# Latent attention on one core: the two score products take three pairs of accumulation banks in turn

## The chip, the cores and the metric

The kernel runs on one core of one Trainium2 chip. The metric is the device time of one execution in microseconds (us). The core has a matmul engine (TensorE, in profiles PE, with its weight loads as PEld), a vector engine (VectorE, DVE), an activation engine (ScalarE, ACT), a general engine (GpSimd, POOL) and a queue for transfers (SyncE, SP).
## The reference, cut to what matters

On a sequence of 2048 tokens by 128 features: half of a six-layer windowed stack, then a latent attention, then the windowed stack again. Only the latent attention is touched.

```python
x = x + 0.5 * _L0_ffn_ref(_layernorm(x), ...)      # six layers, window 32
x = x + _L0_attn_ref(_layernorm(x), ...)           # the latent attention
x = x + 0.5 * _L0_ffn_ref(_layernorm(x), ...)

# _L0_attn_ref, 16 heads; 8 content and 32 rope numbers a head
q = jnp.concatenate([q_content, q_rope], axis=-1)  # 40 numbers a head
k = jnp.concatenate([k_content, k_rope], axis=-1)
scores = jnp.einsum('bhqd,bhkd->bhqk', q, k) * scale
scores = jnp.where(causal[None, None], scores, jnp.float32(-jnp.inf))
attn = jax.nn.softmax(scores, axis=-1)
out = jnp.einsum('bhqk,bhkd->bhqd', attn, v)
return out.transpose(0, 2, 1, 3).reshape(Bx, Tx, N_HEAD * HEAD_DIM) @ W_o
```

## The kernel before

The 16 heads are taken as 8 pairs. The two heads of a pair lie on partitions 0 to 63 and 64 to 127 of `qT` and `kT`: 32 rope rows, one row (32) that holds minus the row maximum in `qT` and one in `kT`, and 8 content rows, so 41 rows in use (`QS = 41`). Rows 41 to 63 were filled once, with 0 in `qT` and with 1 in `kT`, and nothing else writes them. Everything is fp32.

Each pair goes through two score products.

- `scores(pair, y)`, 36 items a pair: queries on the output's partitions, keys along the free axis. VectorE's `maxima` reduces the item to row maxima (line 1455 and neighbours) and signals `s_read`. The maxima of a group of 512 queries are turned into a row by `maxima_turned` and copied to row 32 of `qT`.
- `keyed(pair, t)`, 36 items a pair: the product the other way round, keys on partitions, with minus the maximum already inside. ScalarE's `exps` (line 1374) takes the exponential into `ptl`, four buffers deep, and signals `exped_l`. `outputs` multiplies `ptl` by the values; `summed` normalises a finished group.

An item is one of four kinds: F (a full 128 by 512 block for both heads), D (the diagonal blocks, with the causal mask added by a bf16 matmul first), A and B (the rest of the diagonal group, 384 columns).

Banks before: `keyed` and `exps` use banks 0 to 1 and 2 to 3 in turn (`bank = 2 * (t % 2)`); `scores` and `maxima` have banks 4 and 5 alone, except that the first 18 items of pair 0 (`AHEAD = 18`), before the main loop, go round all three pairs of banks. Bank 6 collects the outputs. Bank 7 is shared by `rope` (line 1170), `maxima_turned` (1211) and `summed` (1280), each of which VectorE must have read before the next may start (`bank_free`).

The order on TensorE is written out by hand. Step t of a pair's 36 issues `keyed(t)`; a rope product for the next pair where t is a multiple of 4 up to 28; `maxima_turned` at t = 5, 19, 22, 29; `summed` at t = 2, 7, 13, 25; `outputs` after t-1 where a unit ends there; and `scores` 18 items ahead. VectorE's order is: rope (three multiplications, lines 1443 and 1446), turned row (1473), normalisation, maxima. ScalarE's is: exps, at t = 1 two long clears of a row (line 1387), copy of a finished group.

The waits of the main loop before: `scores` item n waits until item n-1 is reduced (`s_read`); `keyed` step t waits until exps of step t-2 are done (`exped_l`, which starts at 2); `outputs` at step t waits for the exps of step t-1.

Of the kernel before, what the change touches and what calls it, by code (L numbers as in the profile page):

```python
# [56 lines left out]
QS = QD + 1  # L57
RMS_EPS = 1e-6
PAIRS = HEADS // 2
# [848 lines left out]
def latent_attention(nc, z, i, c, q0, x_res, x_a, x_b, ident, ident_h, causal, mean_w, ones_w, neg_half, zeros):  # L908

    VW = CD + 1  # L910
    with ExitStack() as st:
        def sb(name, shape, dt=F32):
            return st.enter_context(nc.sbuf_tensor(name, shape, dt))
# [28 lines left out]
        ptl = sb("ptl", [P, 4, 2, GT])  # L942
# [29 lines left out]
        NI = 36  # L972
# [3 lines left out]
        AHEAD = 18  # L976
# [32 lines left out]
            return (pair + ahead, y) if pair + ahead < PAIRS else None  # L1009

        def score_bank(pair, y):
            return (4, 0, 2)[y % 3] if pair == 0 and y < AHEAD else 4

        def last_unit(u):
            return u + 1 == len(units) or units[u + 1][0] != units[u][0]
# [90 lines left out]
        def _(pe):  # L1107
# [39 lines left out]
            for n in range(G):  # L1147
# [10 lines left out]
                for m in range(4):  # L1158
                    t = 4 * n + m
# [5 lines left out]
            def rope(pair, j):  # L1165
# [3 lines left out]
                src = qc[:, n * GT:(n + 1) * GT] if w == "q" else x_a[:, 1 + n * GT:1 + (n + 1) * GT]  # L1169
                pe.matmul(ps[:, 7, :], ws[w][:, :], src, start=True, stop=True).then_inc(z["a_ready"], 1)  # L1170

            def heads_rows(h):
                return slice(64 * h, 64 * h + QS)

            def scores(pair, y):
                g, kind = s_items[y][0:2]
                b, bank, early = pair % 2, score_bank(pair, y), pair == 0 and y < AHEAD
                if y == first[g]:
                    pe.wait_ge(z["roped"], pair * 2 * NR + 4 * (g + 1))
                if y == 0:  # L1180
                    pe.wait_ge(z[f"qk_rows_{b}"], 64 * (pair // 2 + 1))
                    if pair >= 1:
                        pe.wait_ge(z["rows_cleared"], 2 * pair)
                if not early:
                    pe.wait_ge(z["s_read"], pair * NI + y)
                elif y >= 3:
                    pe.wait_ge(z["s_read"], y - 2)
                if kind == "D":
                    for h in range(2):
                        pe.matmul(ps[:, bank + h, :], ident_h[:, :], causal[:, :].unsqueeze(1).to_broadcast([P, 4, P]),  # L1190
                                  start=True, stop=False, skip_group_check=True)
                    for t in range(4):
                        for h in range(2):
                            cols = slice((4 * g + t) * P, (4 * g + t + 1) * P)
                            mm = pe.matmul(ps[:, bank + h, t * P:(t + 1) * P], qT[heads_rows(h), b, cols], kT[heads_rows(h), b, cols],
                                           start=False, stop=True, skip_group_check=True)
                else:
                    k0 = s_items[y][3] * GT if kind == "F" else g * GT
                    parts = {"F": lambda: ((s_items[y][2], 0, GT),), "A": lambda: ((4 * g + 1, 0, P), (4 * g + 2, P, 2 * P)),
                             "B": lambda: ((4 * g + 3, 0, 3 * P),)}[kind]()  # L1200
                    for r, lo, w in parts:
                        for h in range(2):
                            mm = pe.matmul(ps[:, bank + h, lo:lo + w], qT[heads_rows(h), b, r * P:(r + 1) * P], kT[heads_rows(h), b, k0:k0 + w],
                                           start=True, stop=True, skip_group_check=True)
                mm.then_inc(z["s_ready_l"], 1)
# [9 lines left out]
            def keyed(pair, t):  # L1215
                b = pair % 2
                g, kind = t_items[t][0:2]
                if t == first[g]:
                    pe.wait_ge(z["m_read"], pair * 2 * G + 2 * (g + 1))
                pe.wait_ge(z["exped_l"], pair * NI + (t + 1))  # L1220
                bank = 2 * (t % 2)
                if kind == "D":
                    for h in range(2):
                        pe.matmul(ps[:, bank + h, :], causal[:, :], ident_h[:, :].unsqueeze(1).to_broadcast([P, 4, P]),
                                  start=True, stop=False, skip_group_check=True)
                    for n in range(4):
                        for h in range(2):
                            cols = slice((4 * g + n) * P, (4 * g + n + 1) * P)
                            mm = pe.matmul(ps[:, bank + h, n * P:(n + 1) * P], kT[heads_rows(h), b, cols], qT[heads_rows(h), b, cols],
                                           start=False, stop=True, skip_group_check=True)  # L1230
                else:
                    parts = {"F": lambda: ((t_items[t][2], 0, 0, GT),), "A": lambda: ((4 * g + 1, 2 * P, 0, 2 * P), (4 * g + 2, 3 * P, 2 * P, P)),
                             "B": lambda: ((4 * g, P, 0, 3 * P),)}[kind]()
                    for kt, q0, lo, w in parts:
                        for h in range(2):
                            mm = pe.matmul(ps[:, bank + h, lo:lo + w], kT[heads_rows(h), b, kt * P:(kt + 1) * P],  # L1236
                                           qT[heads_rows(h), b, g * GT + q0:g * GT + q0 + w], start=True, stop=True, skip_group_check=True)
                mm.then_inc(z["t_ready"], 1)

            def outputs(pair, u):  # L1240
                b = pair % 2
                g, js = units[u]
                pe.wait_ge(z["exped_l"], pair * NI + (js[-1] + 3))
                if u == 0:
                    pe.wait_ge(z["vp_ready"], (pair + 1) * VS)
                if u == 0 or units[u - 1][0] != g:
                    pe.wait_ge(z["osb_ready"], pair * G + (g + 1))

                def add(h, kt, j, src, q0, w, start):
                    strip = 2 * h + kt % 2  # L1250
                    return pe.matmul(ps[32 * strip:32 * strip + 32, 6, q0:q0 + w], vp[:, b, h, kt, :], ptl[:, j % 4, h, src:src + w],
                                     start=start, stop=True, skip_group_check=True)

                for j in js:
                    kind = t_items[j][1]
                    if kind == "F":
                        kt = t_items[j][2]
                        for h in range(2):
                            mm = add(h, kt, j, 0, 0, GT, kt < 2)
                    elif kind == "D":  # L1260
                        if g == 0:
                            for h in range(2):
                                pe.matmul(ps[64 * h + 32:64 * h + 64, 6, 0:P], zeros[:, 0:32], ptl[:, j % 4, h, 0:P],
                                          start=True, stop=True, skip_group_check=True)
                        for n in range(4):
                            for h in range(2):
                                mm = add(h, 4 * g + n, j, n * P, n * P, P, g == 0 and n == 0)
                    elif kind == "A":
                        for n, src, w in ((1, 0, 2 * P), (2, 2 * P, P)):
                            for h in range(2):  # L1270
                                mm = add(h, 4 * g + n, j, src, 4 * P - w, w, False)
                    else:
                        for h in range(2):
                            mm = add(h, 4 * g, j, 0, P, 3 * P, False)
                mm.then_inc(z["pv_part"], 1)
# [9 lines left out]
            def first_rope(j):  # L1285
                if j >= 1:
                    pe.wait_ge(z["rb_ready"], 2 * j)
                if j >= 6:
                    pe.wait_ge(z["m_read"], 2 * (j - 5))
                rope(0, j)  # L1290
# [3 lines left out]
            for y in range(AHEAD):  # L1294
# [5 lines left out]
                    maxima_turned(0, y // 11)  # L1300
                if y in EARLY:
                    first_rope(EARLY[y])
            pe.wait_ge(z["s_read"], AHEAD)

            def bank_free(pair, t, rotated=0):
# [40 lines left out]
        def _(act):  # L1347
# [15 lines left out]

            act.wait_ge(z["lat_spread"], G)
            act.wait_ge(z["lat_kv"], G)
            nc.scalar.copy(ptl[:, 2, 0, 0:1], ident[:, 0:1]).then_inc(z["exped_l"], 1)
            nc.scalar.copy(ptl[:, 3, 0, 0:1], ident[:, 0:1]).then_inc(z["exped_l"], 1)
            nc.scalar.copy(osb[:, 0:1], ident[:, 0:1]).then_inc(z["osb_ready"], 1)

            def exps(pair, t):  # L1370
                w = width[t_items[t][1]]
                bank = 2 * (t % 2)
                act.wait_ge(z["t_ready"], pair * NI + (t + 1))
                nc.scalar.activation(ptl[:, t % 4, :, 0:w], ps[:, bank:bank + 2, 0:w], ACT.Exp, scale=scale).then_inc(z["exped_l"], 1)  # L1374

# [161 lines left out]
```

## Time and profile before

| | |
|---|---|
| time, median of 3 runs | 5177.82 us (5175.47 to 5184.58) |
| profiled execution, time | 5162.74 us |
| profiled execution, span | 5160.7 us |
| share of the span busy: PE, DVE, ACT, POOL | 95%, 74%, 69%, 69% |
| mean granted TensorE clock | 0.960 |

The profile is of one execution. Busy times of PE are modelled at their ends: consecutive matmuls overlap there, and a gap shorter than that overhang does not appear as idle. A line number is a line of the kernel printed above. `ps_l` is the PSUM tensor of the latent attention, `ptl` the exponentials, `rpm` the maxima.

### The profile page before, as it was taken

What the parts mean: (1) busy time and instruction counts of PE and PEld (TensorE: products, weight loads), DVE (VectorE), ACT (ScalarE), POOL (GpSimd) and SP (SyncE); (2) the same over time, 40 slices, a digit from 0 to 9 for tenths busy, and PEclk for the clock granted to TensorE, in tenths of its full rate; (3) what the DMA queues carried; (4) which work ended last, traced back from release to release, by engine and by line L of the source; (5) the groups of instructions that cost most, each with busy time, mean ns of one, the idle gap of its engine ahead of it and who ended that gap; (6) DMA issues with size and microseconds to landing.
All of it is one profiled execution on the core that took longest, in us unless ns stands there. A gap on an engine that the chain in (4) does not pass through costs nothing. (4 is left out here: it accounts for less than half of the span.)

```text
span 5160.7 us, 141547 instructions
## 1 busy us (share of the span) xinstructions
PE 4888.7 (95%) x46192; PEld 3069.9 (59%) x46192; DVE 3801.2 (74%) x8349; ACT 3585.5 (69%) x10733; POOL 3573.1 (69%) x4474
## 2 busy tenths in 40 slices
PE   7999999999999997899999997999999999999998
PEld 4666666666666664334444443666666666666664
DVE  5888888788888884455555544888888888888885
ACT  4888888888888884033333334888888888888885
POOL 6988888888888884211111105988888888888884
PEclk8999999999999998589998998999999999999998
DMA  2122122221222211000000002122121221212211
GB/s 74 46 57 54 45 61 50 56 53 44 61 51 55 53 45 35 5 2 4 3 3 3 3 1 58 47 58 53 44 62 49 55 54 44 62 48 55 56 44 33
DMA packets 296783, 217.39 MB, mean 42 GB/s; under 512 B 81996, under 2 KB 293576, under 8 KB 295112
## 3 DMA queue, kind: packets, MB, share of 16 engines
q1 hardware_dynamic: 296008, 207.74, 16.0%
q8 instruction: 402, 6.59, 0.5%
q14 instruction: 373, 3.06, 0.2%
HBM read 40.83 MB, written 1.05 MB: 8 GB/s over the span
## 5 line engine op out<-in xcount | busy, mean ns | idle before, releaser
L541 POOL TENSOR_TENSOR inv<-ssm,neg_half 128x8 f32<-128x8 f32 x768 | 1365.6, 1778 | 122.3 <-DVE ssm L860 55.0
L555 POOL TENSOR_TENSOR rot<-t 128x256 f32<-128x256 f32 x1536 | 1123.3, 751 | 328.9 <-DVE t L849 260.5
L732 ACT ACTIVATE prob<-ps,nmx,inv 128x96 f32<-128x96 f32 x3072 | 1288.2, 434 | 55.1 <-DVE nmx L846 42.7
L628 PE MATMUL ps<-w_qkv,xs 128*128 128x512 f32 x1536 | 875.2, 652 | 59.6 <-issue 30.4
L1374 ACT ACTIVATE ptl<-ps_l 128x1024 f32<-128x1024 f32 (+1 forms) x288 | 280.0, 977 | 647.0 <-PE ps_l L1236 508.5
L835 DVE TENSOR_REDUCE mx<-ps 128x4 f32<-128x384 f32 x768 | 424.8, 553 | 374.6 <-PE ps L655 371.9
L732 ACT ACTIVATION_READ_ACCUMULATOR prob<-ps,nmx,inv 128x1 f32 x3072 | 632.3, 206 | 0.0
L725 ACT COPY vt<-ps 128x256 f32<-128x256 f32 x768 | 286.4, 373 | 465.1 <-PE ps L666 453.8
L819 DVE TENSOR_TENSOR t<-ps,tab_s 128x256 f32<-128x256 f32 x1536 | 573.7, 413 | 38.7 <-issue 32.1
L827 DVE TENSOR_TENSOR prob<-prob,rec 128x384 f32<-128x384 f32 x768 | 562.8, 733 | 26.4
L716 ACT ACTIVATE sq<-ps 128x512 f32<-128x512 f32 x768 | 472.8, 616 | 111.2 <-PE ps L628 107.7
L856 DVE TENSOR_REDUCE ss<-sq 128x8 f32<-128x512 f32 x768 | 519.2, 676 | 28.5 <-ACT sq L716 27.1
L666 PE MATMUL ps<-w_qkv,xs 128*128 128x256 f32 x1536 | 539.4, 433 | 0.0
L697 PE MATMUL ps<-pt,vs 96*64 96x64 f32 x12288 | 526.4, 228 | 1.9 <-ACT pt L762 1.9
L676 PEld LDWEIGHTS ps<-ident,prob 128*96 128x96 f32 x3072 | 355.8, 127 | 288.7 <-issue 208.0
L849 DVE TENSOR_TENSOR t<-ps,tab_c 128x512 f32<-128x512 f32 x768 | 524.8, 683 | 0.0
L741 ACT COPY qkt<-ps 128x512 f32<-128x512 f32 x768 | 456.9, 595 | 67.8 <-PE ps L683 67.8
L697 PEld LDWEIGHTS ps<-pt,vs 96*64 96x64 f32 x12288 | 420.4, 137 | 130.5 <-issue 127.9
L559 POOL TENSOR_TENSOR rot<-rot,inv 128x256 f32<-128x256 f32 x768 | 472.8, 616 | 0.0
L676 PE MATMUL ps<-ident,prob 128*96 128x128 f32 x3072 | 464.9, 274 | 7.1 <-DVE prob L827 3.4
L683 PE MATMUL ps<-ident,rot 128*128 128x128 f32 x3072 | 462.2, 273 | 2.8 <-POOL rot L559 2.8
L762 ACT COPY pt<-ps 96x512 f32<-96x512 f32 x768 | 460.6, 600 | 0.0
(190 smaller groups left out, 8101.9 us busy)
## 6 DMA issues: line engine op xcount, KB each, us to landing
vs<-vt SPq DMA_DIRECT2D x768, 96.0 KB, 2.2
vs<-vt SPq DMA_DIRECT2D x768, 64.0 KB, 2.0
vs<-vt SPq DMA_DIRECT2D x768, 32.0 KB, 1.8
xs<-x_a SPq DMA_DIRECT2D x384, 32.0 KB, 1.9
w_qkv<-in_L_ffn_Wqkv SPq DMA_DIRECT2D x48, 256.0 KB, 3.8
w_qkv<-in_L_ffn_Wqkv SPq DMA_DIRECT2D x48, 128.0 KB, 3.2
w_o<-in_L_ffn_Wo SPq DMA_DIRECT2D x12, 512.0 KB, 4.4
w<-in_L_ffn_W SPq DMA_DIRECT2D x12, 341.0 KB
```

What stands on the lines that cost most here:

```text
L541: nc.gpsimd.tensor_tensor(inv[:, n % 4], ssm[:, n % 2], neg_half[:, 0:2 * HU], ALU.pow).then_inc(z["inv_ready"], 1)
L555: nc.gpsimd.tensor_tensor(rot[:, n % 4, half[w]], t1[:, n % 2, half[w]], t2[:, n % 2, half[w]], ALU.add).then_inc(z["rotated_" + w], 1)
L559: nc.gpsimd.tensor_tensor(kh, kh, inv[:, n % 4, HU:2 * HU].unsqueeze(2).to_broadcast([P, HU, DH]), ALU.mult).then_inc(z["k_normed"], 1)
L628: pe.matmul(ps[:, j % 2, :], xs[:, j // UT % 2, :], w_qkv[:, 0:2, u * 256:(u + 1) * 256], start=True, stop=True).then_inc(z["qk_ready"], 1)
L666: pe.matmul(ps[:, 6, 0:256], xs[:, n // UT, :], w_qkv[:, 2, (n % UT) * 256:(n % UT + 1) * 256], start=True, stop=True).then_inc(z["v_ready ...
L676: mm = pe.transpose(ps[0:SKEYS, 5, h * P:(h + 1) * P], prob[:, n % 2, h, :], ident[:, :])
L697: mm = pe.matmul(ps[64 * b:64 * b + 64, 6, 256 + r * P + st * STRIP:256 + r * P + (st + 1) * STRIP], vs[0:SKEYS, n, st, h, :], pt[0:SKEYS, ...
L732: e = nc.scalar.activation(prob[:, n % 2, h, :], scores[:, h % 2, h // 2, :], ACT.Exp, scale=inv[:, n % 4, h:h + 1], bias=nmx[:, n % 2, h: ...
L819: nc.vector.tensor_tensor(a[:, :, :, lo:lo + hf], b[:, :, :, hi:hi + hf], sn, ALU.mult).then_inc(z["t2_ready"], 1)
L827: nc.vector.tensor_tensor(prob[:, n % 2], prob[:, n % 2], rec[:, n % 2].unsqueeze(2).to_broadcast([P, HU, SKEYS]), ALU.mult).then_inc(z["w ...
L849: nc.vector.tensor_tensor(heads_qk(t1[:, w % 2]), heads_qk(ps[:, w % 2]), cb, ALU.mult).then_inc(z["t1_ready"], 1)
L856: nc.vector.tensor_reduce(ss[:, j % 2], sq[:, j % 2].rearrange("p (h d) -> p h d", d=DH), X, ALU.add).then_inc(z["summed"], 1)
```

## The change

Both products take the three pairs of banks (4-5, 0-1, 2-3) in turn, in the order in which TensorE issues them: keyed, scores, keyed, scores. So an item reuses the banks of the item three places back in that order. For `keyed` at step s that is the scores item of step s-2, so it waits on `s_read`; for `scores` at step s it is the keyed item of step s-1, so it waits on `exped_l`. After the last scores item `keyed` waits for the exps of step s-3. Both products use 64 rows a head in place of 41. The two one-number copies that gave `exped_l` its start of 2 go, and `outputs` counts without them (the same exps as before). A wait for `s_read` of 18 ahead of the main loop goes.

```diff
+        RING = (4, 0, 2)
+
+        def keyed_bank(pair, t):
+            return RING[(AHEAD + 2 * (pair * NI + t)) % 3]
+
         def score_bank(pair, y):
-            return (4, 0, 2)[y % 3] if pair == 0 and y < AHEAD else 4
+            n = pair * NI + y
+            return RING[(n if n < AHEAD else AHEAD + 2 * (n - AHEAD) + 1) % 3]
...
             def heads_rows(h):
-                return slice(64 * h, 64 * h + QS)
+                return slice(64 * h, 64 * h + 64)
 
             def scores(pair, y):
-                b, bank, early = pair % 2, score_bank(pair, y), pair == 0 and y < AHEAD
+                b, bank, step = pair % 2, score_bank(pair, y), pair * NI + y - AHEAD
...
-                if not early:
-                    pe.wait_ge(z["s_read"], pair * NI + y)
+                if step >= 1:
+                    pe.wait_ge(z["exped_l"], step)
                 elif y >= 3:
-                    pe.wait_ge(z["s_read"], y - 2)
+                    pe.wait_ge(z["s_read"], y - 2 + (step == 0))
...
             def keyed(pair, t):
-                pe.wait_ge(z["exped_l"], pair * NI + (t + 1))
-                bank = 2 * (t % 2)
+                bank, step = keyed_bank(pair, t), pair * NI + t
+
+                if step - 2 < PAIRS * NI - AHEAD:
+                    pe.wait_ge(z["s_read"], step + AHEAD - (2 if step == 0 else 1))
+                else:
+                    pe.wait_ge(z["exped_l"], step - 2)
...
             def outputs(pair, u):
-                pe.wait_ge(z["exped_l"], pair * NI + (js[-1] + 3))
+                pe.wait_ge(z["exped_l"], pair * NI + (js[-1] + 1))
...
-            pe.wait_ge(z["s_read"], AHEAD)
...
-            nc.scalar.copy(ptl[:, 2, 0, 0:1], ident[:, 0:1]).then_inc(z["exped_l"], 1)
-            nc.scalar.copy(ptl[:, 3, 0, 0:1], ident[:, 0:1]).then_inc(z["exped_l"], 1)
...
             def exps(pair, t):
-                bank = 2 * (t % 2)
+                bank = keyed_bank(pair, t)
```

## Rows read from the trace of the kernel before

**Rows 1.** The page: span, busy time by engine, granted clock in 40 slices.
```profile
span 5160.7 us, 141547 instructions
PE 4888.7 (95%) x46192; PEld 3069.9 (59%) x46192; DVE 3801.2 (74%) x8349; ACT 3585.5 (69%) x10733; POOL 3573.1 (69%) x4474
PEclk8999999999999998589998998999999999999998
```

**Rows 2.** Busy time in stretches: busy us and (instructions), clock, DMA share, GB/s.
```profile
2142.00:2207.00 65.00, 58.99 (x218) 25.76 (x218) 39.92 (x48) 2.14 (x3) 19.78 (x18) 0.50 0.00 0
2207.00:3110.00 903.00, 843.38 (x5782) 368.23 (x5778) 489.95 (x616) 320.38 (x329) 150.77 (x136) 0.96 0.01 3
```

**Rows 3.** Who PE waited for in 2207 to 3110: us, times, longest.
```profile
PE ps_l L1203 <- DVE rpm L1455: 27.6, 43, 1.3
PE ps_l L1251 <- ACT ptl L1374: 5.3, 11, 0.6
PE ps_l L1203 <- DVE rpm L1460: 5.2, 9, 0.6
PE ps_l L1280 <- DVE rb L1446: 4.7, 7, 0.9
PE ps_l L1203 <- DVE rpm L1462: 4.7, 7, 0.7
PE ps_l L1211 <- DVE rb L1446: 4.5, 12, 0.4
PE ps_l L1190 <- DVE rpm L1455: 3.8, 8, 0.5
PE ps_l L1203 <- DVE rpm L1457: 2.8, 6, 0.5
```

**Rows 4.** Timeline, clock 1.0: start, duration, engine, line, idle before and releaser.
```profile
2282.08 1.13 PE L1203 MATMUL ps_l<-kT,qT 41*128 41x512 f32 x4
2283.04 1.02 PE L1236 MATMUL ps_l<-qT,kT 41*128 41x512 f32 x4
2283.90 1.02 PE L1170 MATMUL ps_l<-qc,ws_q 64*128 64x512 f32 x2
2287.56 1.07 PE L1280 MATMUL ps_l<-sel,osb 128*128 128x18 f32 x8 [0.93 <-DVE rb L1446]
```

**Rows 5.** Timeline around one long wait of a scores item.
```profile
2228.34 1.02 PE L1170 MATMUL ps_l<-qc,ws_q 64*128 64x512 f32 x2
2229.87 1.13 PE L1203 MATMUL ps_l<-kT,qT 41*128 41x512 f32 x4
2230.83 0.81 PE L1236 MATMUL ps_l<-qT,kT 41*128 41x384 f32 x4
2231.64 1.23 DVE L1455 TENSOR_REDUCE rpm<-ps_l 128x2 f32<-128x1024 f32 x1
2232.91 1.13 PE L1203 MATMUL ps_l<-kT,qT 41*128 41x512 f32 x4 [1.27 <-DVE rpm L1455]
```

**Rows 6.** The clock's longest fall in the main loop, same columns as rows 2.
```profile
2753.10:2770.20 17.10, 17.10 (x64) 6.69 (x58) 4.86 (x8) 3.07 (x3) 1.09 (x1) 0.50 0.00 1
```

**Rows 7.** The same work at the two clocks: timeline of the prelude and the tail.
```profile
2165.74 3.79 PE L1203 MATMUL ps_l<-kT,qT 41*128 41x512 f32 x8
3103.36 1.99 PE L1236 MATMUL ps_l<-qT,kT 41*128 41x512 f32 x8
```

**Rows 8.** Other falls of the clock in the main loop, columns of rows 2.
```profile
2234.40:2248.00 13.60, 13.60 (x42) 3.65 (x38) 4.93 (x6) 3.66 (x4) 0.00 (x0) 0.50 0.00 0
2944.30:2957.90 13.60, 13.60 (x42) 3.64 (x38) 4.86 (x5) 3.66 (x4) 0.12 (x1) 0.50 0.00 0
```

**Rows 9.** Timeline at a pair's step 3: ScalarE's two clears.
```profile
2441.64 3.84 ACT L1387 ACTIVATE qT<-turn 1x2048 f32<-1x2048 f32 x2
2446.36 1.29 PE L1251 MATMUL ps_l<-ptl,vp 128*32 128x256 f32 x10 [0.63 <-ACT ptl L1374]
```

## The prediction

> **What bounds the kernel now.** I read the page first: TensorE is busy 95% of 5160.7 us, and the two windowed stacks fill most slices at full clock; the slices in the middle, where the clock row shows 8, 5, 8, 9, are the latent attention [rows 1]. The change touches only that part, so I cut it out by stretches: a prelude of 65 us (the 18 scores items ahead), all at clock 0.50, and a main loop of about 903 us at mean clock 0.96, with PE busy 843.4 and VectorE 490 (54%) [rows 2]. TensorE is the bound of the main loop, but not without holes. What the loop can lose is (a) PE's waits and (b) the time at half clock. VectorE, at 490 of 903, and ScalarE, at 320, have room.
>
> The list of PE's waits shows who makes the holes [rows 3]. First come scores items (1203, and 1190 where a D item starts with its mask) that wait for the maximum of the item before: 27.6 + 5.2 + 4.7 + 3.8 + 2.8 = 44.1 us in 73 waits. Then come waits of bank 7 (1280 and 1211 behind rope's `rb`): 4.7 + 4.5 = 9.2 us in 19. Then outputs that wait for exps, 5.3 us in 11.
>
> These idle times are too short, by the modelled end of the block before. Unhindered blocks show by how much: a scores block starts at 2282.08 and lasts 1.13, yet the keyed block starts at 2283.04, 0.96 later; the keyed block lasts 1.02 and the next starts 0.86 later [rows 4]. Overhang: 0.17 and 0.16. The scores waits are therefore worth 44.1 + 73 x 0.165 = 56 us.
>
> **The change, part by part.**
>
> *The scores wait goes.* The scores item of step s now needs the exps of step s-1. Between the keyed block of step s-1 and this item stand at least one scores and one keyed block, 0.96 + 0.86 = 1.82 us; a release by the exps takes 1.02 (their duration in the main loop) and about 0.2 for handing over. That is met. The exception is ScalarE's pair of row clears, 3.84 us, at step 1, which delays the exps of step 2: but the outputs of step 3 wait for those exps already (0.63 us) and stand ahead of that step's scores item, so nothing is added [rows 9]. Gain: 56 us.
>
> *The keyed item gets a wait on maxima.* It needs the maximum of the scores item two steps back. Behind it on TensorE stand everything else of the step, and behind its result ScalarE and the outputs. In a step with no rope, the maximum is done 1.23 + 0.3 after its scores block, and TensorE passes a keyed and a scores block first (1.82): met. In the seven or eight rope steps of a pair VectorE has the rope work ahead of the maximum: in the example the rope product starts at 2228.34, and the maximum that it delays runs from 2231.64 to 2232.87 [rows 5]. That is 3.7 us after an unhindered end at 2229.2. TensorE passes scores, keyed and scores by then, 2.8 us, and outputs, about 0.9 where they are full, so only a short or absent outputs block leaves a wait. In the example: scores at 2229.87, keyed at 2230.83, then (no longer held to 2232.91) scores at 2230.83 + 0.64 (384 columns of 512 at 0.86) = 2231.47, and the next keyed would want 2232.43 and gets 2232.9: a wait of 0.5 in place of 1.27 plus overhang. By the written order such a place comes once in each pair (step 9 to 10, after the outputs of a D item). I take 8 x 0.5 = 4 us, and 2 for the small items at a pair's start; the ends are 0 and, if every rope step left 0.7, 55 x 0.7 = 39 us. Value: 6 us, since the other rope steps have a full outputs block.
>
> *Bank 7's waits.* They hang on rope and what stands between it and the next user of bank 7. At 2287.56 the wait is 0.93 with no stall of scores between [rows 4]; it stays. Some of the others were covered by a scores wait: of 61 blocks of 1211 and 1280 in the loop (480/16 and 248/8 matmuls), 19 wait now. If the remaining 42 each waited 0.5 it would give back 21 us. I take 0 and keep 21 for the range; most of them stand a full outputs block behind the rope product.
>
> *Sixty-four rows.* A rope product on 64 rows (2283.90, two matmuls) takes 1.02 us, as the 41-row keyed block of the same 512 columns does [rows 4]. I take 0 for the time of a matmul. Both heads already run side by side (four matmuls in 0.86 us, where the rope product's two alone take as long), so no concurrency is won either. The rows filled with 0 in `qT` add zero to the sums.
>
> *The removed copies, the removed wait ahead of the loop and the tail.* Two copies of one number: below 1 us. The last 18 keyed steps wait for the exps by their outputs as before: 0.
>
> *The clock.* In the main loop the clock falls to 0.5 in seven stretches: four of 13.6 to 13.7 us, two of 3.4, one of 17.1; together 78.5 us [rows 6, 8]. In them PE is busy all the time. Eight matmuls over two blocks take 3.79 us at half clock and 1.99 at full [rows 7], so a microsecond at half clock costs (3.79 - 1.99) / 3.79 = 0.47 us: all falls cost 37 us. Four of them (13.6 + 3.4 + 13.7 + 13.6 = 44.3 us) come within 3 us of exactly the 1.27 us wait of rows 5, repeated in other pairs [rows 5, 8]. If the clock falls because TensorE had stood still before, shortening that stall removes these: 44.3 x 0.47 = 21 us. The other three follow the 0.93 wait of bank 7 and the 0.63 wait of outputs, which stay. I take 21; the ends are 0 and 37. The prelude runs at 0.5 throughout, though PE is busy 59 of 65 us [rows 2]; its waits hardly change, and I take 0 there, with 65 - 40 (VectorE busy) - 5 for hand-overs = 20 us as the other end, if the wider products should bring the clock up early.
>
> A rule that speaks against the change stands in the Trainium skill, "TensorE: Matmul & The Clock Gate", section "A second HAM failure mode: psum-queue depth-cycling": a kernel that cycles through PSUM banks leaves many tiny pauses between groups of matmuls, and the clock swings between its levels. The trace agrees in part: the clock swings with pauses of only 1.27 us, but with `scores` on one pair of banks. By that rule the falls would stay or grow, and the sum would be the waits alone.
>
> **Sum.** 56 - 6 + 21 = 71 us. The profiled execution took 5162.7, 15 below the median of 5177.8; 5162.7 - 71 = 5092 for an execution like it, and against the median 5177.8 - 71 = 5107.
>
> **The rivals.**
>
> 1. Stalls go and half the falls with them (the forecast): 5107, own range 5090 to 5125. Chance 0.45.
> 2. The clock gains more: all falls go and the prelude rises to full clock. For it: the prelude at 0.50 with PE busy 91% shows that being busy is not enough to be granted full speed, and the number of rows at work is something that the change alters. Against it: nothing here shows rows to matter. 56 - 6 + 37 + 20 = 107: 5071. Chance 0.24.
> 3. The falls stay, moved to other places: they depend on alignment, since the 1.27 us wait occurs in every pair and only four times precedes a fall. 56 - 6 = 50: 5128. Chance 0.18.
> 4. The stall moves to bank 7: TensorE arrives sooner at blocks that need the rope bank, whose release hangs on VectorE's 2.1 us of multiplications. 56 - 6 - 21 = 29, and no gain of clock: 5149. Chance 0.07.
> 5. Slower: keyed items inherit the coupling to VectorE. Each of the 55 rope steps leaves a keyed wait as long as the scores wait of rows 5 (1.27): 70 + overhang 55 x 0.165 = 79 given back, 23 more than won: 5201. It decides when the maximum is on average 1.0 us later than TensorE at rope steps (56 / 55); I worked out 0.7 without outputs and none with. Chance 0.04.
> 6. The product waits are replaced by an equal loss, no change: 0.02.
>
> **How the numbers follow.** A measurement of this kernel tells about 0.2% (10 us) from no change. Cases 1 to 4 are faster by more than that: 0.94. Same 0.02, slower 0.04. For eight in ten: below, case 2 with a little more than all (5071 less 7 for a run like the lowest); above, case 3 with part of the bank-7 cost (5128 + 15). Range 5064 to 5143.
>
> **What would show it.** In the profile after: the waits of 1203 and 1190 on `rpm` are gone from PE's list and 1236 has new ones on `rpm`, some 6 to 10 us; PE's wait for `rb` (1280, 1211) is 9 to 20 us; the loop from the first outputs to the last is 50 to 75 us shorter; the clock's mean in it is 0.97 or more; VectorE's busy time is unchanged at 490. The prelude is still 65 us long at 0.50; if it is shorter, case 2 holds. The prediction is wrong if keyed items wait for `rpm` for over 30 us or if more time than 78 us is spent at half clock.

## The result, and the profile after

The changed kernel takes 5065.88 us (median of 4 runs, 5061.69 to 5068.41) against 5178.78 us (4 runs, 5175.47 to 5184.58): a ratio of 0.978, 95% interval 0.9763 to 0.9797, 113 us less. The forecast was 5107 with a range of 5064 to 5143. The time lies inside it by 2 us, at its low edge, below the second rival (5071) and outside the forecast's own narrower range (5090 to 5125).

First the page of the changed kernel: span, busy time by engine, and the clock in 40 slices.

```profile
span 5065.6 us, 141545 instructions
PE 4828.9 (95%) x46192; PEld 3060.8 (60%) x46192; DVE 3798.8 (75%) x8349; ACT 3584.9 (71%) x10731; POOL 3573.6 (71%) x4474
PEclk8999999999999998599999988999999999999998
```

The work of VectorE, ScalarE and POOL is that of before [rows 1]; only TensorE's busy time is 60 us lower, mainly since more of its time is at full clock. In the clock row the slices behind the dip to 5, which hold the main loop, are 9 one after another, up to the one in which the loop ends; before, 8s stood among them.

Next the stretches of the changed kernel: the prelude from the first rope product to the first exps, the main loop from there to the output transposes, and the start of the next stack (columns as in [rows 2]).

```profile
2131.90:2187.70 55.80, 39.94 (x175) 16.03 (x176) 39.41 (x50) 0.00 (x0) 21.95 (x20) 0.76 0.04 8
2187.70:3012.20 824.50, 802.05 (x5874) 366.89 (x5872) 493.34 (x623) 325.16 (x334) 153.32 (x138) 1.00 0.01 3
3012.20:3073.80 61.60, 35.68 (x76) 16.52 (x76) 15.32 (x26) 3.71 (x6) 11.47 (x7) 0.56 0.19 62
```

The same stretches of the kernel before, cut at the same events:

```profile
2132.10:2199.90 67.80, 56.01 (x175) 22.68 (x176) 40.76 (x50) 0.00 (x0) 21.97 (x20) 0.50 0.03 6
2199.90:3117.00 917.10, 855.24 (x5875) 375.02 (x5874) 493.68 (x622) 325.16 (x334) 153.29 (x138) 0.95 0.01 3
```

The prelude is 12.0 us shorter, with its clock at 0.76 instead of 0.50. The main loop is 92.6 us shorter, with its clock at 1.00 instead of 0.95: of the falls one of 3.4 us is left. It begins 1.5 us after TensorE has waited 0.93 us for bank 7 (timeline; 1293 is the sum):

```profile
2686.57 1.07 PE L1293 MATMUL ps_l<-sel,osb 128*128 128x18 f32 x8 [0.93 <-DVE rb L1456]
```

From the output transposes to the end the changed kernel takes 2053.4 us (5065.6 - 3012.2), the one before 2043.7 (5160.7 - 3117.0): 9.7 us longer. So the two profiled executions are 95 us apart and not 113. The code there is the same. Its stretch in the kernel before and in the changed one:

```profile
3117.00:5160.70 2043.70, 1954.56 (x20008) 1320.90 (x20008) 1624.92 (x3821) 1623.42 (x5187) 1688.08 (x2145) 0.98 0.20 52
3012.20:5065.60 2053.40, 1963.22 (x20008) 1325.42 (x20008) 1624.89 (x3821) 1622.94 (x5187) 1688.27 (x2145) 0.97 0.20 52
```

The same 20008 matmuls keep TensorE busy 8.7 us longer; the other engines' busy times agree within 0.7 us. By the traces' clock records 88.7 us of this stretch are at half clock before and 123.3 after. A further profile of the kernel before (below) has 100.2 us at half clock and takes 2047.2; the changed kernel's variants have 93.5 to 125.6 and take 2047 to 2056, by and large the longer the more. So the 9.7 us come with 34.6 us more at half clock behind the loop. Why there is more of it in one execution than in another stays open.

Then who PE waited for in the changed kernel's main loop (2190 to 3010): us, times, longest. Line 1264 is outputs, 1220 the turned row, 1293 the sum, 1249 keyed.

```profile
PE ps_l L1264 <- ACT ptl L1384: 7.4, 12, 1.6
PE ps_l L1220 <- DVE rb L1456: 5.3, 14, 0.4
PE ps_l L1293 <- DVE rb L1456: 4.7, 7, 0.9
PE ps_l L1249 <- DVE rpm L1465: 3.5, 7, 0.5
```

The 73 waits of scores for `rpm` [rows 3] are gone without a successor: no scores line is in the whole list. In their place keyed waits 3.5 us in 7, with the overhang 4.7 (7 x 0.165 more). Bank 7's waits for `rb` are 10.0 us in 21, where they were 9.2 in 19. The place that the prediction walked through [rows 5] looks like this in the changed kernel (timeline):

```profile
2214.11 1.13 PE L1212 MATMUL ps_l<-kT,qT 64*128 64x512 f32 x4
...
2215.07 0.81 PE L1249 MATMUL ps_l<-qT,kT 64*128 64x384 f32 x4
2215.71 1.02 PE L1212 MATMUL ps_l<-kT,qT 64*128 64x512 f32 x4
2215.87 2.36 DVE L1465 TENSOR_REDUCE rpm<-ps_l 128x2 f32<-128x1024 f32 x2
...
2217.24 1.13 PE L1249 MATMUL ps_l<-qT,kT 64*128 64x512 f32 x4 [0.51 <-DVE rpm L1465]
```

The second scores item starts 0.64 after the keyed one, as soon as that has streamed, and the next keyed item waits 0.51 us for the maximum. That is the 0.5 that was worked out, once a pair.

### The profile page after: what moved, and what is told of

The parts are those of the page before. It is cut to its first block and busy times, and to the rows that moved or that the text cites. A ratio compares the mean times of both kernels' runs of the same rounds, so it can differ in the third digit from the quotient of the medians.

```text
span 5065.6 us, 141545 instructions
## 1 busy us (share of the span) xinstructions
PE 4828.9 (95%) x46192; PEld 3060.8 (60%) x46192; DVE 3798.8 (75%) x8349; ACT 3584.9 (71%) x10731; POOL 3573.6 (71%) x4474
## 5 line engine op out<-in xcount | busy, mean ns | idle before, releaser
L856 DVE TENSOR_REDUCE ss<-sq 128x8 f32<-128x512 f32 x768 | 519.3, 676 | 28.3 <-ACT sq L716 26.8
```

Of the source, the lines that this page charges most:

```text
L856: nc.vector.tensor_reduce(ss[:, j % 2], sq[:, j % 2].rearrange("p (h d) -> p h d", d=DH), X, ALU.add).then_inc(z["summed"], 1)
```

## The experiments

Theory A: the clock falls because TensorE stood still for a scores item; the ring of banks gives all of the gain and the rows none. Theory B: how many rows the instructions at work name matters for the clock, so that the two parts of the change each give something. The time of every run but the last is a median of five or six executions; each profile is of one.

**1. The ring alone, 41 rows a head.**

```diff
             def heads_rows(h):
-                return slice(64 * h, 64 * h + 64)
+                return slice(64 * h, 64 * h + QS)
```

> The ring of banks as changed, but 41 rows a head as before. Theory A (the clock falls because TensorE stood still for a scores item; the rows do nothing): the waits on maxima are gone, the falls of the clock in the main loop with them, and only the prelude may be as before: 5066 to 5081 us. Theory B (the number of rows at work is what holds the clock up and lets it rise): the waits are gone (some 56 us), but the prelude stays 65 us long at 0.50 and some of the 78 us of falls in the main loop stay: about 5095 to 5120 us.

Measured: 5105.74 us, ratio 0.9862 (0.9844 to 0.988) to the 5175.75 of the kernel before, timed beside it. The ring alone is worth 70 us. Its prelude and main loop, the loop's first 25.7 us, and one fall of the clock in the loop:

```profile
2124.90:2191.20 66.30, 55.87 (x175) 22.61 (x176) 40.75 (x50) 0.00 (x0) 21.90 (x20) 0.50 0.03 7
2191.20:3042.40 851.20, 831.84 (x5875) 376.20 (x5874) 492.94 (x622) 325.36 (x334) 153.36 (x138) 0.96 0.01 3
2191.20:2216.90 25.70, 25.70 (x114) 11.36 (x117) 10.00 (x13) 10.13 (x9) 4.97 (x4) 0.50 0.00 1
2315.90:2329.60 13.70, 13.38 (x52) 4.78 (x54) 4.76 (x7) 3.82 (x5) 3.10 (x4) 0.50 0.00 0
```

The prelude is all at half clock, and so are the first 25.7 us of the loop (7.2 before). The loop is 851 us where the changed kernel has 824.5. Further on in it stand three falls of 13.7 us. The four falls that followed a long scores wait are gone, as the prediction had it. All three that remain begin at the same place, step 3 of a pair. The timeline there, around the start of the fall at 2315.9 (1397 are ScalarE's row clears, 1264 outputs):

```profile
2311.49 3.84 ACT L1397 ACTIVATE qT<-turn 1x2048 f32<-1x2048 f32 x2
2315.36 1.73 ACT L1384 ACTIVATE ptl<-ps_l 128x768 f32<-128x768 f32 x2
2316.22 0.66 PE L1264 MATMUL ps_l<-ptl,vp 128*32 128x256 f32 x6 [0.63 <-ACT ptl L1384]
```

The fall begins while TensorE waits. Theory A fails for the rows: 27 us of the loop and 11 of the prelude come only with 64, and of the 27 some 12 (25.7 x 0.47) are the loop's slow start.

**2. Sixty-four rows alone, banks as before.**

```diff
             def heads_rows(h):
-                return slice(64 * h, 64 * h + QS)
+                return slice(64 * h, 64 * h + 64)
```

> The kernel before with 64 rows a head and nothing else: banks and waits as before. Theory A: PE's waits on maxima are as before (44 us plus overhang), the falls stay, the time is that of before, 5179 us within 5. Theory B: the waits stay, the falls in the main loop go (37 us) and the prelude is some 15 us shorter: about 5126 us.

Measured: 5126.37 us, ratio 0.9905 (0.989 to 0.9921), 49 us less. Stretches:

```profile
2128.10:2186.10 58.00, 39.95 (x175) 16.03 (x176) 39.80 (x50) 0.00 (x0) 21.98 (x20) 0.77 0.04 7
2186.10:3068.80 882.70, 817.92 (x5875) 364.60 (x5874) 493.61 (x622) 325.17 (x334) 153.22 (x138) 1.00 0.01 3
```

And the longest wait on PE's list for the whole loop:

```profile
PE ps_l L1203 <- DVE rpm L1455: 28.9, 46, 1.3
```

The scores waits are all there (with the other four scores lines of that list 46.1 us in 78), 1.3 us at the longest as before [rows 3], and yet the clock falls only once for 3.4 us inside the loop, after a wait of 0.93 for bank 7. So the standstill is not enough for a long fall: it takes the standstill and 41-row blocks around it.

**3. Fifty-two rows.** The changed kernel with `slice(64 * h, 64 * h + 52)`.

> The changed kernel with 52 rows a head, halfway between 41 and 64. Theory A: the time of the changed kernel, 5066 us. Theory B: the clock's gain is partly there; the time lies between that of the ring with 41 rows and the changed kernel, and the prelude's stretch at 0.5 is longer than the changed kernel's 54 us or equal to it.

Measured: 5070.65 us, ratio 0.9797 (0.978 to 0.9815); five of the six executions took 5062.29 to 5074.35 us and one 5492.54. The loop is 824.4 us at 1.00, as with 64. The prelude is 57.3 us with 38 of it at half clock, against 55.8 with 27.2. So the effect isn't in proportion to the rows; in the loop it is complete at 52. In the prelude the difference is small beside that of one execution to another: run 4, with 64 rows, has 34.6 us at half clock.

**4. The added rows with zeros in both operands.**

```diff
-            fills = [..., (kT[:, :, :], 1.0), (qT[:, :, :], 0.0), ...]
+            fills = [..., (kT[:, :, :], 0.0), (qT[:, :, :], 0.0), ...]
...
+                    nc.gpsimd.memset(kT[RD:RD + 1, :, :], 1.0)
+                    nc.gpsimd.memset(kT[64 + RD:64 + RD + 1, :, :], 1.0)
```

> The changed kernel with 64 rows a head, but with rows 41 to 63 of kT holding 0 instead of 1 (row 32 keeps its 1), so that the added rows carry zeros in both operands; the sums are the same. If the clock follows the rows that an instruction names, the time is that of the changed kernel, 5066 us. If it follows what the rows compute, the time is that of the ring with 41 rows. By theory A it is 5066 us too.

Measured: 5071.12 us, ratio 0.9791 (0.9771 to 0.9811); loop 824.5 us at 1.00, prelude 56.8. It follows the rows that the instructions name; they may hold zeros in both operands. Added rows with other numbers in both were not tried, since they would change the sums.

**5. Which product.** The changed kernel with 41 rows in one of the two.

```diff
+            def used_rows(h):
+                return slice(64 * h, 64 * h + QS)
...              # in keyed (first run) or in scores (second run)
-    kT[heads_rows(h), b, ...], qT[heads_rows(h), b, ...]
+    kT[used_rows(h), b, ...], qT[used_rows(h), b, ...]
```

> The changed kernel, but with 41 rows in keyed and 64 in scores. The prelude holds scores items alone, so if the rows of the instructions at work there let the clock rise, it is as short as the changed kernel's (56 us from the first rope product to the first exps, against 66 with 41 rows in both). In the main loop half of the gain in rows is gone: falls of the clock come back in part or not at all: 5066 to 5090 us. If the clock had nothing to do with rows there, the prelude would be 66 us.

> The mirror: 64 rows in keyed and 41 in scores. The prelude should be 66 us long and at half clock throughout, as in the ring with 41 rows; the main loop as in the run with keyed at 41 rows. 5075 to 5100 us. If the prelude is short here too, its clock does not follow the scores items' rows.

Measured: 5064.98 us with keyed at 41 and 5074.39 with scores at 41; the changed kernel itself, timed beside them, 5064.63. Prelude and loop of the first, then of the second:

```profile
2126.50:2181.20 54.70, 37.43 (x175) 15.01 (x176) 39.41 (x50) 0.00 (x0) 21.93 (x20) 0.81 0.04 8
2181.20:3007.70 826.50, 804.11 (x5875) 367.35 (x5873) 493.20 (x623) 324.87 (x334) 153.05 (x138) 1.00 0.01 3
```

```profile
2136.20:2198.40 62.20, 50.86 (x175) 20.20 (x176) 40.00 (x50) 0.02 (x1) 21.98 (x20) 0.56 0.03 7
2198.40:3025.30 826.90, 804.55 (x5874) 368.44 (x5872) 493.27 (x623) 325.13 (x334) 153.35 (x138) 0.99 0.01 3
```

The prelude, whose items are all of scores but the last, follows their rows: 54.7 us against 62.2. With 41 its clock came up for the last 8 us all the same (0.56, not 0.50 as I expected), and before the first keyed item, so 41 rows do not keep it down without exception; in the four other profiles with 41 rows in scores the prelude is at 0.50 throughout. In the loop one product at 64 rows is enough: 826.5 and 826.9 against 824.5. Of the rows' gain there, 2 us hang on the second product.

**6. The changed kernel again.**

> The changed kernel unaltered, on the same chip as the three others, so that differences of some 10 us can be read: 5066 us, no fall of the clock over 3.4 us in the main loop, prelude 56 us.

Measured: 5064.63 us, ratio 0.9796 (0.978 to 0.9811), loop 824.5, prelude 55.8. The one fall of 3.4 us in its loop stands at the same place as in the first profile.

**7. Bank 7's users away from the rope product.**

```diff
-        TURN = {5: (0, 2), 19: (0, 3), 22: (1, 0), 29: (1, 1)}
-        SUM = {2: (-1, 3), 7: (0, 0), 13: (0, 1), 25: (0, 2)}
+        TURN = {6: (0, 2), 19: (0, 3), 22: (1, 0), 30: (1, 1)}
+        SUM = {2: (-1, 3), 7: (0, 0), 14: (0, 1), 26: (0, 2)}
```

> The changed kernel with four users of bank 7 one step later, away from the rope product: turned rows at steps 6 and 30 in place of 5 and 29, sums at 14 and 26 in place of 13 and 25. The changed kernel's PE waits 4.9 + 4.7 us for rb in 20 waits, 13 us with the overhang of 0.165 each. If these waits are on the path that ends last, they go to near zero and the time falls by 8 to 13 us, to about 5055. The rival: the wait only moves to another block (keyed items that need the turned row a step sooner, or maxima), and the time stays at 5066.

Measured: 5055.86 us, ratio 0.9781 (0.9766 to 0.9796), 8.8 us below the changed kernel of run 6, timed beside it. The intervals of the two ratios overlap, but every run of this one (5052.67 to 5061.15) lies below the fastest of the changed kernel there (5061.48), and the loop of the profile is 816.3 us where it was 824.5. PE's list has no wait for `rb` any more. They were on the path. The fall of 3.4 us is gone with them: this loop has no time at half clock, which accounts for 1.6 of the 8.2 us. Some 13 us had been expected from the waits.

**8. ScalarE's clears apart, too.** On top of run 7:

```diff
-                    if t == 1 and pair + 1 < PAIRS:
-                        for h in range(2):
+                    if t in (12, 14) and pair + 1 < PAIRS:
+                        for h in ((t - 12) // 2,):
```

> The run with bank 7 moved, and ScalarE's two clears of a row moved from step 1 to steps 12 and 14, one each, so that the exps of step 2 are no longer 3.84 us late. PE's wait of outputs for exps at step 3 (0.63 plus overhang, in seven of eight pairs) should go: some 5.5 us, the time 5050. If a clear of 1.9 us delays the exps of steps 13 and 15 enough for a new wait, it stays at 5056.

Measured: 5049.5 us (5046.66 to 5050.4), ratio 0.9757 (0.9743 to 0.977). The best of all versions, 15 to 16 us below the changed kernel. That one was not timed beside it, but the loop, 14.1 us shorter, says much the same. The loop, and all that PE still waits for in it:

```profile
2187.40:2997.80 810.40, 803.36 (x5874) 363.53 (x5872) 493.83 (x623) 325.57 (x334) 152.94 (x138) 1.00 0.01 3
```

```profile
PE ps_l L1249 <- DVE rpm L1465: 3.5, 7, 0.5
PE ps_l L1264 <- ACT ptl L1384: 2.0, 5, 0.9
PE ps_l L1293 <- ACT osb L1388: 0.8, 1, 0.8
PE ps_l L1249 <- DVE qT L1483: 0.2, 1, 0.2
```

TensorE is busy 803.4 of 810.4 us.

**9. The clears apart in the ring with 41 rows.** The edit of run 8 (the clears alone; bank 7's users stay) on the kernel of run 1.

> The ring with 41 rows a head, whose three falls of the clock of 13.7 us each start beside that 0.63 us wait of outputs, with the clears moved as in the run before. If the standstill there brings the clock down, the three falls (41 us at 0.47 = 19 us) and the waits (5.5 us) go: about 5081 us against 5106, with the prelude still 66 us at half clock. If the falls have another cause they stay and the time is about 5100.

Measured: 5081.26 us, ratio 0.982 (0.9804 to 0.9837), where run 1 had 0.9862. The three falls of 13.7 us are gone; two of 3.4 are in the loop. The loop:

```profile
2194.70:3027.00 832.30, 815.58 (x5875) 371.70 (x5874) 492.97 (x622) 325.46 (x334) 153.02 (x138) 0.98 0.01 3
```

832.3 us against 851.2. Without the standstill of outputs, 41-row blocks keep the clock behind the loop's first 26.8 us but for those 6.8: the standstill is necessary for the three falls. With run 2, either is enough to get rid of them: no standstill, or more rows. Both falls of 3.4 begin within 0.9 us of the end of a wait of 0.58 for bank 7.

**10. The kernel before again**, one execution.

> The kernel before, unaltered, for a second profile of it: the profiled execution of before was 15 us below its median. If the stretch after the latent attention differs by chance, it is about as long here as in the changed kernel's profiles (2050 to 2055 us from the first output transpose to the end, against 2044 in the first profile of before), and the prelude and the loop are as in the first profile: 68 and 917 us within the falls of the clock.

Measured: 5166.49 us. Prelude 67.8, loop 913.5 (77.2 us of the window at half clock), the rest 2047.2. So the loop repeats within 4 us, by one fall of the clock more or less, and the rest within 3.5: not as long as the expected 2050 to 2055. One fall here, after a 0.93 wait for bank 7, lasts 20.5 us.

**The pauses before the falls.** In the thirteen profiles every fall of the clock inside the loop begins at most 2.1 us after the end of a wait of TensorE of 0.58 to 1.28 us, or during it. In the five profiles with 52 or 64 rows in both products and bank 7's users as they were, one fall of 3.4 us is left in the loop; with keyed at 41 rows there are two of 3.4, with scores at 41 one of 6.8. Each follows one of the loop's two waits of 0.93 for bank 7, and the two loops without those waits (runs 7 and 8) have no fall. But most waits are followed by none: in run 1 three of the six of 0.63 are.

## Why the prediction was right, and what it mis-sized

- **The scores wait goes, 56 us: right.** No scores line is left on PE's list in the changed kernel or in run 1. Run 2 against the changed kernel has the same rows and nearly the same clock and differs by the ring: loops of 882.7 and 824.5 us, 58.2 us for 56 - 6 = 50 predicted. Of the 8 us more, run 2's own list gives 4: 46.1 us in 78 scores waits, 59 with the overhang, less the keyed waits' 4.7. Another 1 is clock (5.5 us at half clock against 3.4). The last 3 may be waits shorter than the overhang, which the profile doesn't show as idle; that isn't shown.
- **The keyed item's new wait, 6 us: right.** It measures 3.5 us in 7 waits, 4.7 with the overhang, at the place named and of the length worked out (0.51). The slower rival, a keyed wait of 1.27 at each of 55 rope steps, did not come about. The prediction's reason, that a full outputs block behind the rope product gives VectorE its time, fits this, but no run took that block away. One reading on the way is wrong: the unhindered end at 2229.2 is that of the item before. The delayed item started at 2229.87, and an unhindered maximum starts 1.18 after its item (2227.91 after 2226.73 in the same timeline) and lasts 1.23, so it would have ended at 2232.3; the delay is 0.6 us and not 3.7. The example's 0.5 doesn't use that number.
- **Bank 7, 0: nearly right.** 10.0 us in 21 waits against 9.2 in 19; the feared 21 us did not come. That these waits are on the path was shown by moving them (8.2 us of loop, 1.6 of them clock).
- **Sixty-four rows take no time: right.** The durations of the scores matmuls in the changed kernel's loop (min/median/max in ns):

```profile
L1212 PE MATMUL ps_l<-kT,qT x1080: 269/589/693, 2191.5 to 2976.4; 64*128 64x512 f32 x120, 64*128 64x128 f32 x30, 64*128 64x256 f32 x23, 64*128 64x384 f32 x7
```

The same 1080 matmuls with 41 rows, in the kernel before, have the same median; the longest are those at half clock:

```profile
L1203 PE MATMUL ps_l<-kT,qT x1080: 272/589/1220, 2207.2 to 3081.2; 41*128 41x512 f32 x120, 41*128 41x128 f32 x30, 41*128 41x256 f32 x23, 41*128 41x384 f32 x7
```

But from the rows costing nothing I concluded that they gain nothing.
- **The clock, 21 us in the loop and 0 in the prelude: mis-sized.** This is the step that failed. The sum put the rows' effect on the clock at nothing, with no reason but that nothing in the trace spoke for one, and all clock gain on the ring. Run 1 shows what the ring alone does: the four falls that followed a scores wait are gone, as worked out, but so are the two that followed a 0.93 wait of bank 7, and three of 13.7 us stand at the 0.63 wait of outputs where one was. Falls of 78.5 us became 41, and with the loop's first stretch 85.7 us at half clock became 66.6: 9 us gained and not 21. The sentence "The other three follow the 0.93 wait of bank 7 and the 0.63 wait of outputs, which stay" is right about the waits and wrong about the falls: with 64 rows the waits stay (run 2 has even those of scores) and all falls but one of 3.4 us go. The loop before has 85.7 us at half clock (the seven falls and its first 7.2 us), the changed one 3.4: 82.3 x 0.47 = 39 us. The prelude, which the forecast left as it was, gave 12 more.
- **The balance.** In the loop 51 us of waits (56 - 4.7) and 39 of clock are 90, of 92.6 measured; the prelude's 12 make it 105. The profiled executions differ by 95, since the rest is 9.7 longer in the changed one; the medians differ by 113, since the profiled execution of before was 16 below its median.
- **The rivals.** The second rival (chance 0.24) is what happened: all its parts came but the prelude's 20 us, where 12 came, since 27 of its 55.8 us are still at half clock. The sign named for it, a prelude shorter than 65 us, is there, and the loop is 92.6 us shorter where the forecast had 50 to 75. The trace of before had one hint, which I named: a prelude with PE busy 59 of 65 us that never got full clock [rows 2]. It didn't point to the rows; runs 1 and 2 do.
- **How much was luck.** The forecast's 71 us is what the ring alone gives (70, run 1), by terms that were off both ways: waits too low, clock too high. The other 43 us of the 113 are the rows', which the sum had at 0. The range held them, by 2 us, only because it was stretched to the second rival; of two timings of the changed kernel the other (5064.63) lies 0.6 us above the range's lower end.
- **The Trainium skill's rule** in "TensorE: Matmul & The Clock Gate", "A second HAM failure mode: psum-queue depth-cycling", that cycling through banks brings swings of the clock, does not hold here as a rule on banks. The kernel that cycles through three pairs has 41 us of falls at 41 rows (run 1) where the one with a fixed pair for scores has 78.5; at 64 rows both have 3.4 (run 2). Its picture of short pauses does fit: run 9 removed one of 0.63 us a pair and three falls with it.

Additivity: the ring alone gives 70 us, the rows alone 49, together 119, where 113 were measured. Four of the falls can be removed by either, so the parts should overlap; by the loops they do (65.9 + 34.4 = 100.3 for 92.6 together). Timed again beside other runs the changed kernel was 105 us below the kernel before (5064.63 against 5169.71), so 119 and 113 are not to be told apart by the medians.

Left open: why a fall before lasts 13.7 us in one pair and 3.4 in another after the same wait, why some waits bring a fall and others of the same length none, how the number of rows acts on the clock, and why the stretch behind the loop has more time at half clock in one execution than in another.

## What to carry to other kernels

Where two streams of work alternate on TensorE and each is read by another engine, let them share one ring of banks: each then waits on the reader that had a whole step of time, and three pairs do what two and one could not. Before giving a product exactly the rows it needs, try all the rows that its place on the array leaves free (64 a head here): rows filled with zeros in one operand cost no time on TensorE here, and kept its clock up. And look in the stretch before each fall of the clock for a pause, even a short one; moving a long operation of another engine by some steps may remove both.

## What the runs showed of the hardware that I had not expected

- The granted clock depends on the rows that matmuls name. The same prelude of 175 matmuls was at 0.50 throughout in four profiles with 41 rows of 64 in use and at 0.56 in a fifth; with 64 it was at 0.70 to 0.81, with 52 at 0.67. The 0.70 is that with zeros in both operands of the added rows.
- Pauses of 0.6 to 1.3 us in a stream of 41-row blocks were followed, a few times a loop, by 3.4 to 20.5 us at half clock, though TensorE was busy nearly all the time of the fall. With 52 rows or more in both products the same pauses were followed by one fall of 3.4 us, or by none where bank 7's waits were moved.
- A matmul of 64 rows and one of 41 take the same time: median 589 ns over the 1080 scores matmuls of the loop, with either.
